# Three of four whole-array layer norms split into per-tile pieces, the first run during the weight load, and the experts' weights turned before the second cross attention

## The reference, cut to what matters

```
# x, ctx: 64 batches of 64 rows, 128 columns, f32
x = x + tanh(g_xattn[0]) * cross_attention_0(layernorm(x), ctx, ctx)   # 16 heads of 64, 128 memory rows
x = x + tanh(g_ffn[0])   * transformer(layernorm(x))                   # 6 layers: local attention, then FFN
x = x + tanh(g_xattn[1]) * cross_attention_1(ctx, layernorm(x))        # 16 heads of 8
x = x + tanh(g_ffn[1])   * experts(layernorm(x))                       # 8 routed + 2 shared experts, top 2
# layernorm(x) = (x - mean) / sqrt(var + 1e-5) over the 128 columns of each row
```

## Time and profile before

| | |
|---|---|
| median of three runs | 4636.0 us (4634.15 to 4636.34) |
| the profiled execution | 4636.16 us, of which the span is 4634.3 us |
| busy share of PE, DVE, ACT, POOL | 91%, 75%, 55%, 60% |
| x stage, from the first tile's transpose | 65.3 to 709.9 us |
| last FFN ends, l stage begins | 3950.2, 3985.2 us |
| l stage ends, router transposes begin | 4361.0, 4386.4 us |

### The profile page before, as it was taken

One profiled execution on the slowest core, in us unless ns is written; L12 is line 12 of the kernel. 1 busy time (PEld: TensorE's weight loads), 2 busy tenths in 40 slices (PEclk: granted clock), 3 DMA queues, 4 the chain that ended last, 5 costly groups with the idle time before them and its releaser, 6 DMA issues.

```text
span 4634.3 us, 148124 instructions
## 1 busy us (share of the span) xinstructions
PE 4220.5 (91%) x51751; PEld 2916.6 (63%) x51751; DVE 3486.1 (75%) x7330; ACT 2548.2 (55%) x5842; POOL 2803.0 (60%) x3446
## 2 busy tenths in 40 slices
PE   4999996999899988999889998999889998588799
PEld 2777774666656656666656666666666666466565
DVE  3666657999589976999679985999779996566466
ACT  1555554666466654666456663666546664355322
POOL 1333336889288873898468882888648883355200
PEclk9999998999999999999999998999999999688699
DMA  2000000000100001000100001000000001000000
GB/s 80 7 7 7 7 22 11 5 5 6 41 6 4 5 25 23 5 5 7 32 14 5 5 6 42 6 4 5 29 20 5 5 6 26 20 12 12 2 7 11
DMA packets 160436, 64.06 MB, mean 14 GB/s; under 512 B 121364, under 2 KB 155936, under 8 KB 159520
## 3 DMA queue, kind: packets, MB, share of 16 engines
q1 hardware_dynamic: 160288, 62.05, 5.2%
HBM read 26.54 MB, written 2.10 MB: 6 GB/s over the span
## 4 chain that ended last, share of the span: by engine, by line
PE 35%; DVE 29%; issue 25%; ACT 4%; POOL 4%; DVEq 1%; SPq 1%; ACTq 1%; DMA 0%; POOLq 0%
DVE ss L947 6%; DVE big L942 6%; DVE mx L959 5%; PE pj L1463 4%; DVE big L941 3%; DVE e L966 3%; DVE qn L941 3%; PE pj L1306 3%; PE sc L1475 3%; PE turn L1382 3%; PE pp L1264 2%; ACT big L655 2%; PE turn L1463 2%; PE po L1279 2%; PE sc L1622 1%
## 5 line engine op out<-in xcount | busy, mean ns | idle before, releaser
L1364 PE MATMUL pj<-wqkv,xcT 128*128 128x512 f32 x1536 | 830.8, 624 | 23.9 <-DVE big L942 9.0
L647 ACT ACTIVATE big<-pj 128x512 f32<-128x512 f32 x768 | 459.1, 598 | 243.8 <-PE pj L1364 175.8
L506 POOL TENSOR_TENSOR big<-big 128x512 f32<-128x512 f32 x384 | 486.2, 1277 | 142.2 <-DVE big L942 142.2
L942 DVE TENSOR_TENSOR big<-pj,ropes 128x512 f32<-128x512 f32 x768 | 522.1, 680 | 0.0
L506 POOL TENSOR_TENSOR qn<-qn,big 128x512 f32<-128x512 f32 x384 | 486.4, 1276 | 35.0 <-DVE big L942 35.0
L947 DVE TENSOR_REDUCE ss<-big 128x8 f32<-128x512 f32 x768 | 503.9, 677 | 0.2 <-ACT big L647 0.2
L1452 PEld LDWEIGHTS pp<-wo,oT 128*128 128x128 f32 x3072 | 366.9, 196 | 154.5 <-ACT oT L670 154.1
L501 POOL TENSOR_TENSOR e<-e,rc 128x512 f32<-128x512 f32 x384 | 392.9, 1045 | 47.4 <-DVE rc L977 47.4
L1452 PE MATMUL pp<-wo,oT 128*128 128x128 f32 x3072 | 404.0, 286 | 7.0 <-ACT oT L670 7.0
L495 POOL TENSOR_TENSOR qn<-qn,ny 128x512 f32<-128x512 f32 x384 | 397.1, 1046 | 7.5
L495 POOL TENSOR_TENSOR big<-big,ny 128x512 f32<-128x512 f32 x384 | 396.6, 1045 | 7.5
(11 more groups left out here) (298 smaller groups left out, 9587.1 us busy)
## 6 DMA issues: line engine op xcount, KB each, us to landing
wqkv<-in_L_ffn_Wqkv SPq DMA_DIRECT2D x6, 1536.0 KB, 6.4
xsd<-Y SPq DMA_DIRECT2D x192, 32.0 KB
xsd<-Y SPq DMA_DIRECT2D x384, 15.8 KB
xsf<-Y SPq DMA_DIRECT2D x96, 64.0 KB
xsf<-Y SPq DMA_DIRECT2D x192, 31.5 KB
xsx<-Y SPq DMA_DIRECT2D x64, 64.0 KB, 1.8
xsx<-CT SPq DMA_DIRECT2D x64, 64.0 KB, 1.9
wo<-in_L_ffn_Wo SPq DMA_DIRECT2D x6, 512.0 KB, 7.4
```

The lines of the kernel that those rows point to most:

```text
L506: nc.gpsimd.tensor_tensor(U[a.par][i], U[a.par][i], t2b[i % 2], ALU.add).then_inc(sem("d_add"), 1)
L647: nc.scalar.activation(sqb[i % 2], pj[i % 2][:, :], ACT.Square).then_inc(sem("d_sq"), 1)
L942: nc.vector.tensor_tensor(t2v, swapped, sin, ALU.mult).then_inc(sem("d_r"), 1)
L1364: mm(pj[i % 2][:, :], xcT[:, a.par, :], wqkv[:, i * 512:i * 512 + 512], start=True, stop=True).then_inc(sem("d_ch"), 1)
```

## The change

- **Input norm.** X and K are issued first and counted in a semaphore of their own, `x_loaded`. DVE runs `normalise_input` (the old code for the first norm) on it, before it waits for the other weights; scaling of xq and qb follows. SP waits for all loads before the first tile is staged, and per tile for `n_t`.
- **Norm 2** moves into the x stage as a fifth step d: `bn_stats` and `bn_aggr` on DVE, an add and a power on 128x1 on POOL, one `tensor_scalar` on DVE that writes Y and counts `y_ready`.
- **Norm 3** moves into the FFN of the last layer, which gets a program of its own with six steps. Step e_: POOL multiplies Y by the gate and adds X; DVE takes the statistics. Step h: POOL makes the power and normalises (a subtraction and a multiplication on 128x256), and counts `z_ready`.
- **Norm 4** moves into the l stage as a sixth step f, built like step d of the x stage. The router's transposes wait per group of four tiles for `l_y`.
- **Experts' weights.** The three routed weights are loaded while the x stage ends; the shared ones where they were. All eight groups are transposed before the l stage, in two PSUM banks in turn.

The core of the diff:

```diff
-            load(K[:, :], consts)
-            load(X[:, :, :], xd)
+            sp.dma_start(X[:, :, :], xd, ...).then_inc(sem("x_loaded"), 16)
+            sp.dma_start(K[:, :], consts, ...).then_inc(sem("x_loaded"), 16)
...
             def x_tile(t, par):
+                sp.wait_ge(sem("n_t"), t + 1)
...
-            sp.wait_ge(sem("n_y"), 1)
+            sp.wait_ge(s_ld, NLOAD)
...
                 ffn_weights(l)
+                if l == 0:
+                    past(sp, "x_ch", 6 * NT)
+                    for wst, src in ((wst1, w1), (wst3, w3), (wst2, w2)):
+                        sp.dma_start(wst, src.rearrange("e i d -> i e d")).then_inc(sem("exp_loaded"), 16)
...
             def l_tile(t, par):
+                past(sp, "z_ready", t + 1)
# POOL
+            def rsqrt(i, n, name, count):
+                nc.gpsimd.tensor_tensor(n_eps(i, n), n_var(i, n), eps1[:, 0:n], ALU.add).then_inc(sem(name), 1)
+                past(pool, name, count + 1)
+                nc.gpsimd.tensor_tensor(n_rstd(i, n), n_eps(i, n), nhalf[:, 0:n], ALU.pow).then_inc(sem(name), 1)
...                                  # x_body, between probs(c, 3) and probs(b, 0)
+                if d:
+                    past(pool, "x_ag", d.g + 1)
+                    rsqrt(d.par, 1, "x_nr", d.g * 2)
...                                  # f_body, behind the power of step a
+                if e_:
+                    rows = bass.ds(e_.t * FT, FT)
+                    pool.wait_ge(sem("y_ready"), e_.g * FT + (NT + FT))
+                    nc.gpsimd.tensor_tensor(Y[:, rows, :], Y[:, rows, :], tg[:, 1:2]..., ALU.mult).then_inc(sem("z_x"), 1)
+                    past(pool, "z_x", e_.t * 2 + 1)
+                    nc.gpsimd.tensor_tensor(X[:, rows, :], Y[:, rows, :], X[:, rows, :], ALU.add).then_inc(sem("z_x"), 1)
+                if h:
+                    past(pool, "z_ag", h.t + 1)
+                    rsqrt(FT * h.par, FT, "z_nr", h.t * 2)
+                    nc.gpsimd.tensor_tensor(xsd[:, :, :], X[:, rows, :], bc(..., D), ALU.subtract).then_inc(sem("z_c"), 1)
+                    past(pool, "z_c", h.t + 1)
+                    past(pool, "z_nr", h.t * 2 + 2)
+                    nc.gpsimd.tensor_tensor(Y[:, rows, :], xsd[:, :, :], bc(n_rstd(k, FT), D), ALU.mult).then_inc(sem("z_ready"), FT)
...                                  # l_body, between the X add (L567) and the product of step c (L573)
+                if f:
+                    past(pool, "l_ag", f.g + 1)
+                    rsqrt(f.par, 1, "l_nr", f.g * 2)
# DVE
...                                  # x_body: first in the round
+                if d:
+                    past(dve, "x_res", d.g + 1)
+                    nc.vector.bn_stats(n_st(d.par), X[:, d.t, :]).then_inc(sem("x_st"), 1)
                 plus_bias("q", 0)
                 row_max(0, 0)
+                if d:
+                    past(dve, "x_st", d.g + 1)
+                    nc.vector.bn_aggr(dif[:, ...], n_st(d.par)).then_inc(sem("x_ag"), 1)
...                                  # x_body: last in the round
+                if d:
+                    past(dve, "x_nr", d.g * 2 + 2)
+                    nc.vector.tensor_scalar(Y[:, d.t, :], X[:, d.t, :], n_mean(d.par), n_rstd(d.par), ...).then_inc(sem("y_ready"), 1)
...                                  # f_body: behind the copy of var (L1037)
+                if e_:
+                    past(dve, "z_x", e_.t * 2 + 2)
+                    for i in range(FT):
+                        last = nc.vector.bn_stats(n_st(FT * e_.par + i), X[:, e_.t * FT + i, :])
+                    last.then_inc(sem("z_st"), 1)
                 gated(2)
+                if e_:
+                    past(dve, "z_st", e_.t + 1)
+                    past(dve, "z_ready", e_.t * FT - FT)
+                    ... bn_aggr for two tiles, then z_ag
...                                  # l_body: statistics behind max2(0), bn_aggr behind max2(1), at the end:
+                if f:
+                    past(dve, "l_nr", f.g * 2 + 2)
+                    nc.vector.tensor_scalar(Y[:, f.t, :], X[:, f.t, :], ...).then_inc(sem("l_y"), 1)
# PE, in front of the l stage
+            pe.wait_ge(sem("exp_loaded"), 6 * 16)
+            for i, some in enumerate(TURN4):
+                if i >= 2:
+                    pe.wait_ge(sem("w_c"), i - 1)
+                ... four transposes into w_turn[i % 2], w_T
+            pe.wait_ge(sem("y_ready"), NT * (DEPTH + 1))
             stream(pe, NT, l_body, 0, 0, 5, 4)
             past(pe, "l_res", NT)
-            ... the same transposes through one bank, each behind w_c
-            pe.wait_ge(sem("n_y"), 4)
...                                  # router transposes
+                past(pe, "l_y", 4 * i + 4)
```

More of the change, by code:

```diff
@@ L86, in build, with n_st, n_mean, n_var @@
         nhalf = const("half")
+        eps1 = const("eps")
+        def n_st(i):
+            return st[:, 16 + i, :]
+        def n_mean(i):
+            return dif[:, 16 + 2 * i:17 + 2 * i]
+        def n_var(i, n=1):
+            return dif[:, 17 + 2 * i:17 + 2 * (i + n) - 1:2]
+        def n_eps(i, n=1):
+            return m2[:, 16 + i:16 + i + n]
+        def n_rstd(i, n=1):
+            return rstd[:, 16 + i:16 + i + n]
         xq = sb("xq", [P, INNER])
@@ L187, in build @@
         s_ld = sem("loaded")
-        loads = [0]
+        NLOAD = 24 * 16
         ATT_LOADS = 4 * 16
@@ L247, in build @@
         h_banks = [pj, [pt_, pp]]
+        w_turn = [pt_, pp]
         r_turn = [pt_, pp, pj[0], pj[1]]
@@ L459, in _ @@
             nc.gpsimd.memset(l_la[:, :], 0.0).then_inc(sem("l_la0"), 1)
-            head_start(pool, "l_ga", "l_os", "l_km", "l_xb", "l_z", "x_p", "d_un", "d_pr", "d_add", "d_nt", "f_eps", "f_rstd")
+            head_start(pool, "x_nr", "z_x", "z_c", "z_nr", "z_ready", "l_nr", "l_ga", "l_os", "l_km", "l_xb", "l_z", "x_p", "d_un", "d_pr", "d_add", "d_nt", "f_eps", "f_rstd")
             nc.gpsimd.memset(xsd[:, :, :], 0.0)
@@ L465, in _, with x_body @@
             pool.wait_ge(sem("hT_one"), 1)
-            pool.wait_ge(s_ld, NLOAD)
-            rsqrt_many(1)
-            def x_body(n, a, b, c):
+            pool.wait_ge(sem("x_loaded"), 2 * 16)
+            pool.wait_ge(sem("n_var"), 1)
+            nc.gpsimd.tensor_scalar(var[:, :], var[:, :], EPS, None, ALU.add).then_inc(sem("n_eps"), 1)
+            pool.wait_ge(sem("n_eps"), 1)
+            nc.gpsimd.tensor_tensor(rstd[:, :], var[:, :], nhalf, ALU.pow).then_inc(sem("n_rstd"), 1)
+            def x_body(n, a, b, c, d):
                 def probs(tile, s):
@@ L798, in _ @@
                 for j, (k, ex) in enumerate(some):
-                    last = nc.scalar.copy(expert_T(k, ex), pt_[:, j * P:j * P + P])
+                    last = nc.scalar.copy(expert_T(k, ex), w_turn[i % 2][:, j * P:j * P + P])
                 last.then_inc(sem("w_c"), 1)
             act.wait_ge(sem("g_T"), 1)
-            nc.scalar.copy(egT[:, :], pp[:, 0:NE]).then_inc(sem("g_c"), 1)
+            nc.scalar.copy(egT[:, :], w_turn[len(TURN4) % 2][:, 0:NE]).then_inc(sem("g_c"), 1)
+            act.wait_ge(sem("zeroed"), 3)
+            stream(act, NT, l_body, 0, 0, 5, 4)
             for i in range(0, 8, 2):
@@ L1037, in f_body, with layer @@
                     nc.vector.tensor_copy(var[:, 0:FT], dif[:, 1:2 * FT:2]).then_inc(sem("f_mv"), 1)
-                gated(2)
-            with dve.Fori(0, DEPTH) as l:
+                if e_:
+                    past(dve, "z_x", e_.t * 2 + 2)
+                    past_waits(dve, "went_on")
+                    for i in range(FT):
+                        last = nc.vector.bn_stats(n_st(FT * e_.par + i), X[:, e_.t * FT + i, :])
+                    last.then_inc(sem("z_st"), 1)
+                gated(2)
+                if e_:
+                    past(dve, "z_st", e_.t + 1)
+                    past(dve, "z_ready", e_.t * FT - FT)
+                    past_waits(dve, "went_on")
+                    for i in range(FT):
+                        k = FT * e_.par + i
+                        last = nc.vector.bn_aggr(dif[:, 16 + 2 * k:18 + 2 * k], n_st(k))
+                    last.then_inc(sem("z_ag"), 1)
+            def layer(l, final):
                 dve.wait_ge(sem("att_loaded"), l * ATT_LOADS + ATT_LOADS)
@@ L1054, in _, with l_body @@
                 dve.wait_ge(sem("ffn_loaded"), l * FFN_LOADS + FFN_LOADS)
-                stream(dve, NF, f_body, l * NF, l * (NF // 2), 4)
-            dve.wait_ge(sem("y_ready"), NT * (DEPTH + 1))
-            normalise(3, True)
-            def l_body(a, b, c, d, e_):
+                stream(dve, NF, f_body, l * NF, l * (NF // 2), 6 if final else 4)
+            with dve.Fori(0, DEPTH - 1) as l:
+                layer(l, False)
+            layer(DEPTH - 1, True)
+            def l_body(a, b, c, d, e_, f):
                 def max1(h):
@@ L1086, in l_body @@
                 max2(0)
+                if f:
+                    past(dve, "l_res", f.g + 1)
+                    past_waits(dve, "went_on")
```

(5 more changed lines are left out.)

111 lines of the change are left out of this document (52 added, 59 removed).

## The result

The changed kernel takes 4563.3 us (median of four runs) against 4636.2 in the same session: the ratio is 0.984, 95% interval 0.9827 to 0.9852. The forecast was 4574. Its profiled execution took 4562.6 us, the span 4560.5, so 73.8 us of the span are gone where 61.9 were forecast. The ratios in this document leave out one execution of one run (e1), which took 5853 us at a granted clock of 0.65.

A forecast was written before the change was run, and what follows sets the result against it. PE, busy 91% of the span, was taken to stand still about 25 us at each of four norms. Savings less prices summed to -61.9 us, so 4636.2 became 4574; range 4560 to 4590, with rivals 4546 to 4603.

The forecast's parts named there:

- The three terms of norms 1, 2 and 4: PE's pauses at the input norm, norm 2 and norm 4 would shrink, saving 24.8, 23.0 and 25.3 us.
- the term of norm 4: Between the l stage's last X and the router's first transpose: PE goes on almost at once, saving 25.3 us.
- The loop in the last FFN: DVE and POOL wait for each other each round: 6.9 us instead of 4.38, costing 27.7 us over eleven intervals.
- The first leg: Last FFN, from DVE's copy of var to the next round's first write (fxn): 4.0 us, before 1.6.
- the second leg: Last FFN, from fxn to the next copy: 2.4 to 2.8 us, plus 0.4 for fxn being held up.
- The tail: Behind the last FFN copy, POOL finishes norm 3; ACT's first l copy after 25 us instead of 48.3, saving 23.3.
- The prices in x and l: Norm pieces added to the rounds of both stages: 0.1 us a round in x, 0.15 in l; 3 and 4.8 us.
- The FFN did stall: Answers the rival that the last FFN doesn't stall: rounds of 5.0 us, 4553 or 4545 us in all; chance 0.15.
- the rival's 21: Rival that PE's clock falls in the last FFN: rounds of 8.8 us, 21 us more, 4599 in all; chance 0.2.
- the middle way: Within the rival of a falling PE clock: some last-FFN rounds at either clock level, called the likelier; no size given.
- The third rival: Slower than before: per-tile pieces sit on the x and l loops' paths, 1.6 us a round, 4670 us; chance 0.05.
- The input norm lay under the loads: Answers the rival that the input norm isn't under the loads, X late or DVE slowed: 4599 us; chance 0.05.

The follow-up runs named there:

- e1: Changed kernel with VectorE's third gate product moved ahead of its wait and sums in the last FFN: 4553.1 us, 0.9811 of before.
- e4: Changed kernel with VectorE again waiting for all 24 weight loads ahead of the input norm: 4586.0 us, 0.9883 of before.
- e7: Changed kernel with norm 4 again one whole block behind the l stage, experts' transposes still ahead of that stage: 4586.5 us, 0.989 of before.
- e9: Changed kernel with norm 4 whole and the experts' transposes behind the l stage, both together: 4583.1 us, 0.9887 of before.
- e2: Changed kernel with GpSimd's two combination operations put ahead of its epsilon and power in the last FFN: 4536.6 us, 0.9775 of before.
- e5: Changed kernel with VectorE writing each normalised tile twice in both cross attentions (x and l stages): 4577.3 us, 0.986 of before.
- e11: Second run, for its trace, of the changed kernel with each normalised tile written twice in both cross attentions: 4580.8 us.
- e6: Changed kernel with the experts' transposes and their copies again behind the l stage, norms still split: 4566.9 us, 0.9836 of before.

## Why the prediction was right, and where its sizes were off

**The seams.** The three terms of norms 1, 2 and 4 came within 0.5 us each. They were read from one kind of row, what lies between two landmarks on TensorE, less what is left for the last tile. e4 shows the first by undoing it, e7 and e9 the last; norm 2's was not undone and rests on the rows before and after. One thing the term of norm 4 did not say: its 25.3 us hold two edits, and the one with the transposes has a share only through the other. The place where it stood, "the experts' transposes are gone from this place", costed their removal at nothing, and their new place was right to be costed at nothing too: TensorE has turned them before GpSimd ends its tail.

**The loop in the last FFN.** The mechanism was as forecast: copy, epsilon and power, combination, sums, and round again. The first leg, copy to the next write of `fxn`, was forecast at 4.0 us and is 3.94 and 4.24 in turn, 4.04 in the mean. The mis-sized term is the second leg, from `fxn` to the next copy: I had 2.4 to 2.8 and another 0.4 for `fxn` being held up, and it took 2.2 to 2.5 with `fxn` at 0.60 to 0.90 instead of 0.59, and 3.07 and 3.10 in the two rounds at the lower clock. A round was 6.49 us, not 6.9, and eleven of them 4.5 us cheaper. e2 is the proof of the loop: only GpSimd's order changed, and the rounds fell to 4.81. e1, which should have shortened the loop by 0.46 us, left it as it was; the loop has waits of VectorE for itself that other work had covered.

**The tail.** From the last copy to ACT's first l copy I had 25 us and it took 23.3. GpSimd came to its last count 21.7 us behind the copy and not 22.8 (its steps are 3.64 us apart, forecast at 3.8), and the clearing took 1.5 us and not 1.7.

**The prices in x and l.** Forecast 3 and 4.8 us, measured 0.1 and 0.3, though between two traces of one kernel these stages differ by 4 to 5 us, so the measured figures say "small" and no more. The step that failed in x is the one that took the gap in front of line 864 for the reserve. The write of Y did take 0.77 us in most rounds where it takes 0.34 alone, as line 921 takes 0.98 where it takes 0.34 alone. The Trainium skill (SBUF — State Buffer, "Who interferes with whom") has such operations and GpSimd's lock each other out for a whole instruction; with that rule the trace agrees, with a median of 769 ns against a minimum of 343. But even twice that work cost 0.07 us a round, and 0.2 at the very most, with TensorE busy for 98.5% of that stage. For l there is no such answer: 0.15 us a round was taken from the gap of 0.91 in front of line 1063, the measured 0.01 is far inside the scatter, and e5 and e11, which would have shown the gap, changed TensorE's clock as well.

**The rivals.** The FFN did stall, at 6.49 us and not at 5.0. TensorE's clock fell there only in part: to 0.95 over the window of the rounds (busy 51.7 of 69 us), against 1.00 before:

```profile
3843.00:3912.00 69.00, 51.71 (x278) 40.61 (x277) 37.52 (x163) 20.57 (x42) 43.13 (x81) 0.95 0.11 28
```

Most of it ran at 2.4 GHz, though TensorE paused in every round. The fall sits in the last four rounds, at 0.82, 0.93, 0.82 and 0.93; the second trace of the changed kernel has it elsewhere (0.77 in round 9, 0.80 in round 13, 0.96 in the last). It cost 1.7 us here and not the rival's 21. The Trainium skill (TensorE: Matmul & The Clock Gate, Part 1) has throttling as the default and activity as what releases it; the middle way that I drew from it, some rounds at either level, is what the trace shows, at a small price. The third rival, work on the paths of x and l, came to 0.4 us over 64 rounds where 62 were needed, which is less than two traces of one kernel differ by. The input norm lay under the loads.

**The sum.** Of the 11.9 us between the forecast and the profiled result, 7.4 are the two prices, 4.5 the FFN's rounds and 1.7 its tail; the other way go 1.6 us in the experts' stage and 0.4 at the input norm. The prices and the experts' stage are no larger than the scatter between traces (4 to 5 us in x and in l, 1.6 in the experts' stage), so only the rounds and the tail are sizes that the prediction can be said to have missed. The forecast isn't right by errors that cancel: all the larger ones have the same sign, and their whole sum fits into the stated 4560 to 4590, near its lower end.

## What to carry to other kernels

When work of another tile is put into two engines' rounds, walk once around: what does each queue wait for, and can the work in front of that wait only start behind something of the same round? Put what has been ready for a round first on its queue; here that order alone was worth 18.5 us between the landmarks, and the split without it nothing. A gap in front of an instruction is not a stage's reserve; ask whether the engine that paces the stage would notice. And undo two edits at one seam one by one and together, since each may be hidden under the other.

## What the runs showed of the hardware that was not expected

One and the same kernel went through its second cross attention in 375.0 and in 380.1 us, and through its first in 644.3 and 640.1, and was done at the same time. With equal products the l stage's length went with TensorE's granted clock, from 367.9 us at 0.82 to 401.9 at 0.71; TensorE's own busy time held all of the difference. A few microseconds in a stage with pauses in each round therefore need more than one trace before they are an edit's.

A loop between two engines can hide TensorE's lower clock or not. In the changed kernel two rounds at 0.82 were 0.8 us longer than their like at 1.00, with VectorE waiting 0.72 us for TensorE's products in the one looked at; in e1, rounds at 0.78 and 0.72 took 6.18 us, as at 1.00.

Work that is put in front of a stage can give part of its time back through the clock: 8.0 us of transposes ahead of the router cost 4.7 in e6's trace, where the router's groups ran at a granted clock of 0.68 instead of 0.50.
